# Diffusion and convolution of the next quad placed between the LSTM steps of the current one

## The chip, the cores and the metric

The kernel runs on one core of a Trainium2 chip. The metric is the device time of one execution in microseconds (us), as the median of several runs. All arithmetic is fp32; products that matter are made from two fp32r halves ("high" and "low"), three matmuls each.

## The reference

`x` holds 16 graphs (called batches below) of 512 nodes with 128 features, `adj` is one 512 x 512 matrix. Four layers follow each other; each ends with `x = layernorm(x + layer(x))` over the features.

```
L0: h = x @ fc.T + b;  8 times: h += (1/8) * (alph/2 * (adj @ h - h) + h @ w_eff - h + x0)
L1: h = relu(adj @ (x @ Wg0 + bg0));  h = relu(adj @ (h @ Wg1 + bg1))
    for p in 1..4: windows of p successive nodes go through an LSTM of their own
                   (Wih[p-1], Whh[p-1]); its last state replaces the window's last node
L2: graph convolution, linear 128->256, batchnorm, relu, linear 256->128, batchnorm
L3: edge attention with 4 heads over 256 edges, softmax by source node, W_out
```

L0 to L2 work on `x` as it comes out of the layer before. L0 and L1 need nothing of the other batches; L2's batchnorm needs all of them.

## The kernel before

A batch lies in the tile `X` as four chunks of 128 nodes. Four batches are a quad, and there are four quads. Each phase is a block with a barrier at its end.

1. `phase_operators` (L85) loads everything and makes the powers of the diffusion operator, `LT` and `E`, so that the eight Euler steps become one polynomial.
2. `phase_diffusion` (L651) does L0 for all quads. For each batch it turns `X` over and multiplies it with two powers of the operator (Y, 4 PSUM tiles), then combines these with `E` (B, 4 tiles). For each quad come two Horner steps over four batches at once (T and S, 4 tiles each). All eight PSUM banks are one ring. ScalarE (ACT) copies the high part of each tile out, VectorE (DVE) subtracts for the low part and frees the bank. GpSimd (POOL) makes low parts of what lies in SBUF and the scales of layernorm.
3. `phase_recurrent` (L888) does L1. Its weights are transposed and split once and stay in SBUF. The two graph convolutions go through a ring of four banks (4 to 7); the LSTM uses banks 0 to 3, one for each gate.
4. `phase_batchnorm` and `phase_attention` do L2 and L3.

**The LSTM of a quad** has 22 steps, numbered here from 0: four for p = 1 (one for each batch, 512 columns), then for p = 2, 3, 4 two half quads times p time steps (512, 340 and 256 columns). On TensorE (PE) a step has two parts. `from_input` multiplies the split input (`xh`, `xl`) with the input weights, and `from_state` (only for t > 0) the split state (`hh`, `hl`) with the state weights. ACT evaluates the gates, DVE makes the cell and the state. The split input of step k + 1 is made while step k runs: ACT copies `xh` at the start of its part of step k (`split_h`, L1220; where step k + 1 begins a new p, after two of the gates), POOL then subtracts for `xl`, and PE waits for it ahead of `from_input(k + 1)`.

**What sets the order.** The order of each engine's work is written out by `schedule` (L1004). It puts pieces of the convolution of the next quad between `from_input(k)` and `from_state(k)` (for t = 0 behind the step), as many pieces as the list `FILL` says; a piece is one chunk's product, of which four make a tile:

```
FILL = [1, 2, 3, 1, 2, 4, 1, 5, 3, 3, 1, 0, 1, 4, 3, 2, 0, 0, 0, 1, 1, 0]
```

Each engine does its queue strictly in that order, and waits at its semaphores in it. The residual and the second layernorm of a quad run in steps 0 to 6 of the next: statistics at step 3, scales on POOL behind the split for step 5, and the application on DVE at step 6. Quads 1 and 2 are passes of a hardware loop; quads 0 and 3 are written out.

Of the kernel before, what the change touches and what calls it, by code (L numbers as in the profile page):

```python
# [6 lines left out]
ALU = mybir.AluOpType  # L7
# [77 lines left out]
def phase_operators(nc, sh, d):  # L85
# [13 lines left out]
    with ExitStack() as ctx:  # L99
# [46 lines left out]
        sel = sb("sel", [P, C, NE])  # L146
        ones = sb("ones", [P, P])
# [7 lines left out]
                 "u_done", "xh_done", "i_in", "iota_done", "perm_done", "g_done", "deg_done",  # L155
# [25 lines left out]
        def _(sp):  # L181
# [8 lines left out]
            for q in range(sh.NB // QB):  # L190
                for c in range(C):
                    sp.dma_start(sh.X[:, c, q * QB:(q + 1) * QB, :], xv[:, c, q * QB:(q + 1) * QB, :])\
                        .then_inc(S["x_in"], 16)
            sp.wait_ge(S["x_in"], 16 * C * (sh.NB // QB))

        @block.gpsimd
        def _(pool):
# [17 lines left out]
            for c in range(C):  # L215
                pool.wait_ge(S["xh_done"], c + 1)
                low_part(pool, sh.Xl[:, c, :, :], sh.X[:, c, 0:QB, :], sh.Xh[:, c, :, :])

        @block.scalar
        def _(act):  # L220
# [34 lines left out]
        def _(dve):  # L255
# [140 lines left out]
            dve.tensor_copy(sh.ss[:, :, :], bank("PERM").rearrange("p (j e) -> p j e", j=2)).then_inc(S["dve_tile"], 1)  # L396
            low_bias("T'", 1)
            dve.wait_ge(S["dve_tile"], at["T'"] + 1)
            for c in range(C):
                ins = dve.tensor_scalar(Gs[:, c, :], sh.ss[:, 0, :], sh.ioc[:, c:c + 1], None, ALU.is_equal)  # L400
            ins.then_inc(S["g_done"], 1)
            for c in range(C):
                dve.tensor_scalar(Gd[:, c, :], sh.ss[:, 1, :], sh.ioc[:, c:c + 1], None, ALU.is_equal)
# [16 lines left out]
            copy("DROW", sh.drow[:, :], bank("DROW"))  # L420
# [230 lines left out]
def phase_diffusion(nc, sh, d):  # L651
# [3 lines left out]
    C, D, N = sh.C, sh.D, sh.N  # L655
    NQ = sh.NB // QB
    with ExitStack() as ctx:
        sb, sem = allocators(nc, ctx)
        Xh, Xl = sh.Xh, sh.Xl
        norm = sh.norm  # L660
        yh = sb("yh", [P, 2, BABY, N], F32R)
        yl = sb("yl", [P, 2, BABY, N], F32R)
        B2h = sb("B2h", [P, C, QB, D], F32R)
        B2l = sb("B2l", [P, C, QB, D], F32R)
        B01 = sb("B01", [P, C, QB, 2, D])
        tq = sb("tq", [P, C, QB, D])
        th = sb("th", [P, C, QB, D], F32R)
        tl = sb("tl", [P, C, QB, D], F32R)
        names = ("pe_tile", "dve_tile", "hi_done", "xh_done", "xl_done", "xb_done", "th_done", "tl_done",
                 "sum2", "stat_done", "norm_own", "rstd_done", "x1_done")  # L670
        S = {n: sem("d_" + n) for n in names}

        work = [("B", 0), ("Y", 2), ("B", 1), ("Y", 3), ("B", 2), ("B", 3), ("Y+", 0), ("T", 0), ("Y+", 1),
                ("S", 0)]
        TILES = 4 * len(work)
        HEAD = 8
        HIS = {"Y": 3, "Y+": 3, "B": 4, "T": 0, "S": 0}  # L680
        HI_QUAD = sum(HIS[k] for k, _ in work)
        HI_HEAD = 6

        def steps(g, last):

            hi = 0
            for i, (kind, b) in enumerate(work):
                if not (last and kind == "Y+"):
                    skipped = sum(k == "Y+" for k, _ in work[:i]) if last else 0
                    yield kind, b, HEAD + g * TILES + 4 * (i - skipped), 4 * (i - skipped) % 8, \  # L690
                        HI_HEAD + g * HI_QUAD + hi
                    hi += HIS[kind]

        block = ctx.enter_context(nc.Block())

        def ready(eng, n, k):

            eng.wait_ge(S["pe_tile"], n + k + 1)

        @block.tensor  # L700
        def _(pe):
            def free(n, k, first=False):

                if not first:
                    pe.wait_ge(S["dve_tile"], n + k - 7)

            def Y(b, n, bk, first=False):
                for k in range(4):
                    free(n, k, first)
                    o = sh.psum[:, bk + k, :]  # L710
                    if k < 2:
                        src = (Xh, Xl)[k]
                        for c in range(C):
                            ins = pe.transpose(o[:, c * P:(c + 1) * P], src[:, c, b, :].bitcast(F32),
                                               sh.ident[:, :])
                    else:
# [1581 lines left out]
```

## Time and profile before

| | us |
|---|---|
| median of 3 runs (1188.17 to 1189.53) | 1189.31 |
| the profiled execution: span | 1186.6 |
| what lies around the span (median less span) | 2.7 |
| PE busy | 998.1 |
| DVE busy | 665.5 |
| ACT busy | 584.8 |
| POOL busy | 361.7 |

The profiled execution is known by its span, from the first to the last instruction; 2.7 us lie between that and the median of the runs shown. "Busy" for PE is modelled from the starts of matmuls. The stages in the span are: operators 0 to 89.3, diffusion 89.3 to 385.4, set-up and first convolution of the recurrent phase to 433.0, its four LSTM quads to 541.6, 653.6, 769.8 and 873.9, then batchnorm and attention to 1186.6.

### The profile page before, as it was taken

The page shows a single profiled execution, that of the slowest core. Times are in us where ns is not written, and L with a number is a line of the kernel's source. Part 1 is how long each engine was busy: PE and PEld are TensorE (multiplying, and loading weights), DVE is VectorE, ACT ScalarE, POOL GpSimd, SP SyncE. Part 2 cuts the span into 40 slices and gives each one's busy share as a digit, 9 for nine tenths or more (in the row PEclk, how much of TensorE's full clock was granted, in tenths as well). Part 3 has the DMA queues.
Part 4 walks back from the last instruction along what each step waited for, and adds up shares of the span by engine and source line. Part 5 has one row for each costly group of instructions (what it writes and reads, how often), then busy time and mean ns, then how long its engine had stood idle before and what let it go on. Part 6 is the DMA issues. An engine that isn't in the chain of part 4 may idle for free. (4 is left out here: it accounts for less than half of the span.)

```text
span 1186.6 us, 15771 instructions
## 1 busy us (share of the span) xinstructions
PE 998.1 (84%) x5056; PEld 830.2 (70%) x5056; DVE 665.5 (56%) x1422; ACT 584.8 (49%) x1215; POOL 361.7 (30%) x480
## 2 busy tenths in 40 slices
PE   4989999999997788998899789968878966468694
PEld 2678989899896666886688568846856743346483
DVE  4832242342424454677567656756784478744686
ACT  2112314325241375666467646664646567664356
POOL 0021124132221322124322332242224335553156
PEclk9989999999999899999999889987898989689797
DMA  7000000000000300000000000000000000000004
GB/s 190 1 1 1 1 1 0 0 0 0 0 1 1 70 1 1 1 1 1 1 1 1 1 0 0 1 0 1 1 16 1 0 1 1 1 1 0 1 17 127
DMA packets 28700, 13.07 MB, mean 11 GB/s; under 512 B 8032, under 2 KB 27616, under 8 KB 28640
## 3 DMA queue, kind: packets, MB, share of 16 engines
q1 hardware_dynamic: 27680, 12.28, 4.1%
q8 instruction: 28, 0.46, 0.2%
q14 instruction: 32, 0.26, 0.1%
q10 hardware_dynamic: 960, 0.07, 0.1%
HBM read 8.15 MB, written 4.19 MB: 10 GB/s over the span
## 5 line engine op out<-in xcount | busy, mean ns | idle before, releaser
L1252 ACT ACTIVATE gates<-psum,gbias 128x256 f32<-128x256 f32 (+2 forms) x312 | 158.2, 564 | 55.5 <-PE psum L67 54.8
L65 PE MATMUL psum<-xh,WIh 128*128 128x256 f32 (+2 forms) x312 | 117.5, 377 | 56.3 <-POOL xl L72 53.0
L72 POOL TENSOR_TENSOR xl<-Hq,xh 128x256 fp32r<-128x256 f32 (+2 forms) x72 | 74.7, 1038 | 248.1 <-ACT xh L1233 248.1
L65 PEld LDWEIGHTS psum<-xh,WIh 128*128 128x128 f32 x312 | 63.5, 204 | 80.9 <-POOL xl L72 73.0
L67 PE MATMUL psum<-xh,WIl 128*128 128x256 f32 (+2 forms) x312 | 109.9, 352 | 0.0
L66 PE MATMUL psum<-xl,WIh 128*128 128x256 f32 (+2 forms) x312 | 109.7, 352 | 0.0
L647 ACT ACTIVATE X<-X,nshift,nscale 128x128 f32<-128x128 f32 (+1 forms) x180 | 72.0, 483 | 21.4 <-POOL nshift L587 21.4
L1256 ACT ACTIVATE tc<-cell 128x512 f32<-128x512 f32 (+2 forms) x88 | 45.2, 513 | 54.0 <-DVE cell L1345 42.7
L67 PEld LDWEIGHTS psum<-xh,WIl 128*128 128x128 f32 x312 | 63.9, 205 | 5.9
L66 PEld LDWEIGHTS psum<-xl,WIh 128*128 128x128 f32 x312 | 64.1, 205 | 4.4
L781 ACT ACTIVATE yh<-psum 128x512 fp32r<-128x512 f32 x48 | 28.6, 599 | 73.8 <-PE psum L67 72.9
L67 PE MATMUL psum<-Eh,yl 128*128 128x384 f32 x192 | 64.3, 335 | 0.0
L65 PE MATMUL psum<-Eh,yh 128*128 128x384 f32 x192 | 64.3, 335 | 0.0
L66 PE MATMUL psum<-El,yh 128*128 128x384 f32 x192 | 64.2, 334 | 0.0
L72 DVE TENSOR_TENSOR yl<-psum,yh 128x512 fp32r<-128x512 f32 x32 | 22.1, 692 | 67.8 <-ACT yh L781 67.8
L65 PE MATMUL psum<-hh,WHh 128*128 128x256 f32 (+2 forms) x192 | 59.8, 311 | 0.0
L67 PE MATMUL psum<-hh,WHl 128*128 128x256 f32 (+2 forms) x192 | 59.8, 311 | 0.0
L66 PE MATMUL psum<-hl,WHh 128*128 128x256 f32 (+2 forms) x192 | 59.8, 311 | 0.0
L72 DVE TENSOR_TENSOR B2l<-psum,B2h 128x128 fp32r<-128x128 f32 x64 | 18.6, 291 | 72.6 <-ACT B L801 70.2
L607 DVE BATCH_NORM_STATS2 nstats<-X 128x6 f32<-128x128 f32 (+1 forms) x256 | 56.4, 284 | 3.1 <-DVE X L850 1.3
L800 ACT ACTIVATE B2h<-psum 128x128 fp32r<-128x128 f32 x64 | 17.8, 278 | 74.6 <-PE psum L67 74.6
L1339 DVE TENSOR_TENSOR cell<-gates 128x512 f32<-128x512 f32 (+2 forms) x40 | 28.7, 718 | 38.5 <-ACT gates L1252 37.8
(390 smaller groups left out, 2947.6 us busy)
## 6 DMA issues: line engine op xcount, KB each, us to landing
X<-in_x SPq DMA_DIRECT2D x16, 256.0 KB, 5.1
out<-X SPq DMA_DIRECT2D x32, 128.0 KB, 1.9
A<-in_adj SPq DMA_DIRECT2D x1, 1024.0 KB, 6.3
whh<-in_L_gnn_Whh SPq DMA_DIRECT2D x1, 768.0 KB, 8.8
O<-in_L_gnn_W SPq DMA_DIRECT2D x2, 128.0 KB, 2.2
ir<-in_L_gnn_src SPq DMA_DIRECT2D x1, 128.0 KB, 6.1
ir<-in_L_gnn_dst SPq DMA_DIRECT2D x1, 128.0 KB, 6.5
Wg<-in_L_gnn_Wg SPq DMA_DIRECT2D x2, 64.0 KB, 1.9
```

What stands on the lines that cost most here:

```text
L65: pe.matmul(out, lhs[0], rhs[0], start=start, stop=False)
L66: pe.matmul(out, lhs[0], rhs[1], start=False, stop=False)
L67: return pe.matmul(out, lhs[1], rhs[0], start=False, stop=stop)
L72: return eng.tensor_tensor(out, full, high.bitcast(F32), ALU.subtract)
L607: return dve.bn_stats(self.stats[:, bass.ds(self.sh.C * n + c, 1), :], self.sh.X[:, c, bass.ds(n, 1), :])
L647: ins = act.activation(row, row, ACT.Identity, bias=shift[:, k:k + 1], scale=scale[:, k:k + 1])
L781: act.activation(yh[:, b % 2, r, :], sh.psum[:, bk + k, :], ACT.Copy)\
L800: act.activation(B2h[:, c, b, :], sh.psum[:, bk + c, 2 * D:3 * D], ACT.Copy)
L1252: act.activation(gates[:, gate, 0:n], sh.psum[:, gate, 0:n], ACT.Tanh if gate == G else ACT.Sigmoid, bias=gbias[:, p_ - 1, gate:gate + 1]) ...
L1256: act.activation(tc[:, 0:n], cell[:, s % 2, 0:n], ACT.Tanh).then_inc(S["tanh_done"], 1)
L1339: dve.tensor_tensor(c_, gates[:, I, 0:n], gates[:, G, 0:n], ALU.mult).then_inc(S["c_done"], 1)
```

## The change

`phase_diffusion` and `phase_recurrent` become one `phase_main`, with one order of work for all engines, unrolled without loops. A prologue does diffusion and convolution of quad 0, with the transposing of weights between. Then, for quad q, 22 groups that make up diffusion and convolution of quad q + 1 stand one at each LSTM step. Quad 3 has no filling. The diffusion works by pairs of batches, in the same ring of four banks as the convolution.

```diff
+        def taps(q, b):
+            return [("xt", q, b)] + [("y", q, b, r, c) for r in (1, 2) for c in range(C)] \
+                + ([("xs", q, b + 1)] if b < QB - 1 else [])
+        def back(q, b):
+            return [("b", q, b, c) for c in range(C)] + [("xb", q, b)]
+        def giant(kind, q, a):
+            made = [(kind, q, a, j) for j in (0, 1)]
+            return made + ([("th", q, a)] if kind == "t" else [("st1", q, a)])
+        def mix(q, b, layer):
+            return [("c", q, b, layer, c) for c in range(C)]
+        def weigh(q, b, layer):
+            return [("v", q, b, layer)] + ([("relu", q, b)] if layer == 0 else [])
+        def convolve(q):
+            return [[("xs", q, 4)] + mix(q, 0, 0) + [("xs", q, 5)], giant("s", q, 1),
+                    mix(q, 1, 0) + [("ln1", q, 1)] + weigh(q, 0, 0), mix(q, 0, 1) + weigh(q, 1, 0),
+                    mix(q, 1, 1) + weigh(q, 0, 1) + [("ap1", q, 1), ("xs", q, 6)], mix(q, 2, 0) + [("xs", q, 7)],
+                    weigh(q, 1, 1) + mix(q, 3, 0), weigh(q, 2, 0) + mix(q, 2, 1), weigh(q, 3, 0) + weigh(q, 2, 1),
+                    mix(q, 3, 1), weigh(q, 3, 1)]
+        def groups(q):
+            return [[("xs", q, 0)] + taps(q, 0), back(q, 0), taps(q, 1), back(q, 1), giant("t", q, 0), taps(q, 2),
+                    giant("s", q, 0), back(q, 2) + [("ln1", q, 0)], taps(q, 3), [("ap1", q, 0)] + back(q, 3),
+                    giant("t", q, 1)] + convolve(q)
+            for k_ in range(NS):
+                late = {2: [("r", q_ - 1, 0), ("r", q_ - 1, 1)], 3: [("r", q_ - 1, 2), ("r", q_ - 1, 3)],
+                        5: [("st2", q_ - 1)], 6: [("ln2", q_ - 1)], 8: [("ap2", q_ - 1)]}.get(k_, []) if q_ else []
+                middle = [("L", q_, k_)]
+                order += [("X", q_, k_)]
+                order += filling[k_] + late + middle if steps[k_][1] else middle + filling[k_] + late
...
@@ POOL, item xb
+            def add_bias(q, b):
+                n = QB * q + b
+                pool.wait_ge(S["ring_free"], ring["b", q, b, C - 1] + 1)
+                xb = sh.X[:, :, n, :]
+                pool.tensor_tensor(xb, xb, sh.bias0[:, :, :], ALU.add).then_inc(S["xb_bias"], 1)
+                pool.wait_ge(S["xb_bias"], n + 1)
+                pool.tensor_tensor(xb, xb, B01[:, :, b % 2, 0, :], ALU.add).then_inc(S["xb_done"], 1)
@@ POOL, item th
+            def giant_low(q, a):
+                for j in (0, 1):
+                    pool.wait_ge(S["th_done"], 2 * (2 * q + a) + j + 1)
+                    low_part(pool, B2l[:, chunks(j), :, :], B01[:, chunks(j), :, 1, :], B2h[:, chunks(j), :, :])
@@ POOL, item L
+                elif kind == "L":
+                    q, k = at
+                    if k < NS - 1:
+                        split_h(q, k + 1)
@@ PE, items t and s
+            def horner(kind, q, a, j):
+                n = ring[kind, q, a, j]
+                if kind == "t" and j == 0:
+                    pe.wait_ge(S["ring_free"], ring["b", q, 2 * a + 1, C - 1] + 1)
+                if kind == "s" and j == 0:
+                    pe.wait_ge(S["tl_done"], 2 * (2 * q + a) + 2)
@@ SP, the weights (512 KB a load)
+            for q in range(NQ):
+                sp.wait_ge(gate_mm[O], NS * q + end_step(1))
+                load("WI", 2)
+                if q == NQ - 1:
...
+                    sp.dma_start(sh.A[:, :, :], d["adj"].rearrange("(c p) m -> p c m", p=P)).then_inc(sh.a_again, 16)
+                sp.wait_ge(gate_mm[O], NS * q + end_step(2))
+                load("WI", 3)
+                load("WH", 1)
+                sp.wait_ge(gate_mm[O], NS * q + end_step(3))
+                if q < NQ - 1:
+                    load("WI", 0)
+                load("WH", 2)
@@ phase_batchnorm, SP
+            sp.dma_start(sh.ss[:, :, :].rearrange("p j e -> p (j e)"), sh.edges.broadcast_to([P, 2 * sh.NE]))\
+                .then_inc(S["ss_in"], 16)
+            sp.dma_start(sh.drow[:, :], sh.degrees.broadcast_to([P, N])).then_inc(S["drow_in"], 16)
@@ phase_batchnorm, DVE, ahead of its first instruction
+            dve.wait_ge(S["drow_in"], 16)
```

The items: `xs` splits one batch of X (ACT copies, POOL subtracts; one buffer, used by four diffusion and four convolution splits a quad), `xt` and `y` are the three tiles of Y (X is turned over once, not its two halves), `b` the four tiles of B, `xb` the bias and the lowest term, now on POOL, `t`, `s` and `th` the Horner steps of a pair and the split between them, `st1`, `ln1`, `ap1` statistics, scales and application (ACT) of the first layernorm of a pair, `c` and `v` the products with `adj` and with the weights, `relu` and `r` as before, `st2`, `ln2`, `ap2` the second layernorm. `X` and `L` are `from_input` and `from_state`. In the prologue DVE waits for all set-up loads, the biases `bi` and `bh` (the last two of SP's eight) among them, ahead of its first item. Of the seven weight blocks two input ones and one state one have a place in SBUF; all are written to DRAM in the prologue and loaded again for each p. `adj` is overwritten by the states of even quads and loaded again in quad 3. The edge rows and the degree row go through DRAM.

## Rows read from the trace of the kernel before

**Rows 1.** Windows: stretch, length, busy PE, PEld, DVE, ACT, POOL, clock, DMA, GB/s
```profile
89.30:385.40 296.10, 289.60 (x1472) 257.52 (x1473) 99.51 (x224) 94.84 (x253) 71.92 (x83) 1.00 0.00 0
385.40:433.00 47.60, 39.51 (x199) 32.04 (x199) 24.93 (x46) 21.89 (x46) 11.75 (x18) 0.89 0.21 44
433.00:541.60 108.60, 98.39 (x541) 83.21 (x542) 64.85 (x114) 72.44 (x139) 29.77 (x26) 0.97 0.00 1
541.60:653.60 112.00, 98.53 (x553) 83.24 (x552) 77.52 (x153) 69.63 (x139) 36.74 (x39) 0.98 0.00 1
653.60:769.80 116.20, 102.61 (x552) 86.08 (x551) 77.55 (x153) 69.86 (x138) 36.76 (x39) 0.94 0.00 0
769.80:873.90 104.10, 78.70 (x408) 67.67 (x406) 69.43 (x139) 61.26 (x123) 29.14 (x34) 0.85 0.00 1
873.90:1186.60 312.70, 221.89 (x1047) 169.61 (x1047) 201.94 (x450) 177.95 (x353) 137.85 (x216) 0.86 0.06 15
```

**Rows 2.** The same view, of one stretch that holds only B products
```profile
102.07:108.24 6.17, 6.17 (x37) 6.14 (x36) 1.57 (x4) 2.26 (x7) 0.00 (x0) 1.00 0.00 1
```

**Rows 3.** Waits, 433 to 874 us; columns: total us, times, longest
```profile
PEld psum L65 <- POOL xl L72: 73.0, 57, 5.3
```

**Rows 4.** Timeline around step 6, second quad; columns: start, us, then what
```profile
582.52 0.39 PE L65 MATMUL psum<-hh,WHh 128*128 128x512 f32 x1
...
582.72 0.60 ACT L1272 ACTIVATE ych<-psum 128x512 fp32r<-128x512 f32 x1 [7.89 <-PE psum L67]
...
583.21 0.66 ACT L1233 ACTIVATE xh<-Hq 128x512 fp32r<-128x512 f32 x1
...
583.95 1.31 POOL L72 TENSOR_TENSOR xl<-Hq,xh 128x512 fp32r<-128x512 f32 x1 [6.63 <-ACT xh L1233]
...
585.32 0.50 PE L65 MATMUL psum<-xh,WIh 128*128 128x512 f32 x1
```

**Rows 5.** Timeline of PE at step 16, `from_state` to the next step
```profile
633.44 0.28 PE L65 MATMUL psum<-hh,WHh 128*128 128x256 f32 x1
...
634.86 0.28 PE L65 MATMUL psum<-xh,WIh 128*128 128x256 f32 x1
```

**Rows 6.** Timeline where POOL makes sixteen scales ahead of a split
```profile
567.77 0.69 POOL L572 TENSOR_TENSOR nwork<-nstats 128x16 f32 x1
...
576.03 1.29 POOL L72 TENSOR_TENSOR xl<-Hq,xh 128x512 fp32r<-128x512 f32 x1
...
576.11 5.14 DVE L626 TENSOR_SCALAR X<-X,nscale,nshift  x16 [1.94 <-POOL nshift L587]
...
577.37 0.50 PE L65 MATMUL psum<-xh,WIh 128*128 128x512 f32 x1 [3.71 <-POOL xl L72]
```

**Rows 7.** Timeline of POOL: scales of eight columns, first and last
```profile
1171.56 0.21 POOL L572 TENSOR_TENSOR nwork<-nstats 128x8 f32<-128x8 f32 x1
...
1175.65 0.20 POOL L587 TENSOR_TENSOR last_shift<-last_mean,nwork 128x8 f32<-128x8 f32 x1
```

**Rows 8.** Timeline at the start of the second quad
```profile
547.14 2.70 POOL L72 TENSOR_TENSOR rXl<-X,rXh 128x512 fp32r<-128x512 f32 x2 [1.93 <-ACT rXh L1214]
...
548.47 0.50 PE L65 MATMUL psum<-ATh,rXh 128*128 128x512 f32 x1 [0.80 <-POOL rXl L72]
```

**Rows 9.** Groups by line and form, diffusion; busy us, mean ns, idle before
```profile
L801 ACT ACTIVATE B<-psum 128x256 f32<-128x256 f32 x64 | 24.5, 382 | 0.0
...
L647 ACT ACTIVATE X<-X,nshift,nscale x32 | 12.5, 483 | 0.0
```

**Rows 10.** DMA issues of the page; KB each, us to landing
```profile
whh<-in_L_gnn_Whh SPq DMA_DIRECT2D x1, 768.0 KB, 8.8
```

**Rows 11.** Timeline of the queue of SP, last issue of the recurrent set-up
```profile
392.76 3.74 SPq L1089 DMA_DIRECT2D bh<-in_L_gnn_bhh  x1
```

**Rows 12.** Timeline of DVE: one product beside a running POOL split, one alone
```profile
549.82 1.81 DVE L1339 TENSOR_TENSOR cell<-gates 128x512 f32<-128x512 f32 x1
...
561.54 0.69 DVE L1339 TENSOR_TENSOR cell<-gates 128x512 f32<-128x512 f32 x1 [0.40 <-ACT gates L1252]
```

More of the change, by code:

```diff
@@ new lines, in phase_main @@
+        order = prologue()
+        for q_ in range(NQ):
+            filling = groups(q_ + 1) if q_ < NQ - 1 else [[] for _ in range(NS)]
+            assert len(filling) == NS
+            for k_ in range(NS):
[4 more added lines that the diff above has]
+                order += filling[k_] + late + middle if steps[k_][1] else middle + filling[k_] + late
@@ new lines, in phase_main @@
+        order += [("r", NQ - 1, b) for b in range(QB)]
+        ring, high = {}, {}
+        for item_ in order:
+            kind_ = item_[0]
+            if kind_ in ("xt", "b", "t", "s", "v", "r"):
+                name_ = item_
+            elif kind_ in ("y", "c") and item_[4] == C - 1:
+                name_ = item_[:4]
+            else:
+                continue
+            ring[name_] = len(ring)
+            if kind_ in ("xt", "y", "b", "c"):
+                high[name_] = len(high)
@@ L1284, in _ @@
[L1284 to L1285 removed]
+                act.wait_ge(S["c_done"], NS * q + k + 1)
+                act.activation(tcs[:, 0:n], cell[:, s % 2, 0:n], ACT.Tanh).then_inc(S["tanh_done"], 1)
             act.wait_ge(S["g_in"], 64)
             for i in (0, 1):
[L1288 to L1291 removed]
@@ L1292, in _ @@
-            run(schedule(0, True, False), 0, True)
-            with act.Fori(1, NQ - 1) as g:
-                run(schedule(g, True, True), g, True)
-            run(schedule(NQ - 1, False, True), NQ - 1, False)
+                act.activation(Wgs[i][0][:, :], Wg[i], ACT.Copy).then_inc(S["wg_hi"], 1)
+            for item in order:
+                kind, at = item[0], item[1:]
+                if kind == "set":
+                    set_up(*at)
+                elif kind == "xs":
+                    split_x(*at)
+                elif kind == "xt":
+                    taps_high(*at, 0)
+                elif kind == "y" and at[-1] == C - 1:
+                    taps_high(*at[:3])
+                elif kind == "b":
+                    combined(*at)
+                elif kind == "th":
+                    giant_high(*at)
+                elif kind == "ap1":
+                    apply_first(*at)
+                elif kind == "c" and at[-1] == C - 1:
+                    conv_high(*at[:3])
+                elif kind == "relu":
+                    conv_relu(*at)
+                elif kind == "first":
+                    split_h(0, 0)
+                elif kind == "L":
+                    lstm(*at)
```

1091 lines of the change are left out of this document (497 added, 594 removed).

## The prediction

> **What bounds the kernel now.** I read the windows by stage first [rows 1]. Diffusion is PE alone: 289.6 us of 296.1 busy at clock 1.00, so about 74.0 us a quad, and nothing waits. The LSTM quads are different. Quads 0 to 2 take 108.6, 112.0 and 116.2 us with PE busy for 98.4, 98.5 and 102.6; the last, without filling, takes 104.1 with 78.7 busy and a clock of 0.85. ACT, the next engine, is busy for 70 us a quad. So PE bounds the filled quads too, less its waits, and the waits view says which: in 433 to 874 us PE's weight loads wait 73.0 us in 57 cases for `xl` of POOL [rows 3]. This is the wait ahead of `from_input(k + 1)`.
>
> The timeline shows how that wait is made. At [rows 4] a filling ends in a finished tile at 582.5. ACT copies the tile out first, then makes `xh`, then POOL makes `xl` (1.31), and `from_input` starts at 585.32: 2.8 us after the filling's end. PE is not idle there only because `from_state` with 512 columns takes just these 2.80 us. With 256 columns it takes 1.42 [rows 5], and the same chain (0.2 to ACT, 0.5 for the tile, 0.7 for `xh`, some 0.9 for a shorter `xl`) takes 2.3. Where POOL has something else ahead of `xl`, PE waits for that as well: sixteen scales (8.3 us from 567.77 to 576.03) ahead of a split cost PE 3.7 us idle [rows 6].
>
> What the filling can win is therefore what PE idles now: 10.2, 13.5 and 13.6 us in the filled quads, 25.4 in the last. What it can lose is new waits of PE, since every engine keeps its order and PE now has filling enough that any wait is time.
>
> **Work of PE.** Diffusion brings 289.6/4 = 72.4 us a quad. X is turned over once instead of twice: 16 transposes fewer, at most 0.17 each by the larger product of [rows 2] (6.17/36), so I take 2 off: 70.4. The Horner steps by pairs are twice as many products of 256 columns; 1.42/12 = 0.118 [rows 5] against half of 2.80/12 = 0.233 [rows 4], no difference. Three filled quads: 299.5 + 3 x 70.4 = 510.7 us of PE, against 3 x 74.0 + 336.8 = 558.9 us of span now. If no wait were left, 48 us would be won there.
>
> **Waits of a filled quad.** I walk along PE with durations from the rows: an eviction of 512 columns by ACT 0.6 (0.5 start to start), one b tile 0.7 (0.38 of it for the lower terms [rows 9]) and 1.54 on PE [rows 2], DVE's low part 0.7 (0.3 for a b tile), POOL 1.3 for 512 elements [rows 4, 6], 1.1 and 0.9 for narrow ones, 4.3 for eight scales [rows 7], 0.39 for one application by ACT (12.5/32) [rows 9], 5.1 for sixteen by DVE [rows 6].
>
> - Step 0. The first split of X of the next quad stands behind the tanh of step 0. Now POOL begins it 547.14 - 541.6 = 5.5 us after the quad's first product, two chunks in 2.7, and PE starts on it at 548.47 [rows 8]. With 1.3 for one batch it is there at 6.8; PE has 2.1 + 0.4 to do. Wait 4.3.
> - Step 6 to 7. `ln2` stands ahead of the split on POOL, as in [rows 6], with more of PE's work beside it: 2.0 (nothing to 3.7).
> - Step 7 to 8. Behind the last b tile come ACT 0.9, DVE 0.3, then on POOL two bias additions 2.6, `ln1` 4.3, and only then `xl` 1.1: 9.2 us, against 2.8 of `from_state`. Wait 6.4.
> - Step 10. The first t tile needs the last b tile freed. From the last y tile: evictions 1.4, `ap2` on DVE 5.1, the cell and tanh of step 9 1.2, `ap1` on ACT 3.1, four b evictions 2.4, DVE 0.4: 13.6, against 1.4 + 6.2 + 1.8 on PE. Wait 4.2.
> - Step 10 to 11. Behind the last t tile: DVE 0.9, ACT, POOL's two low parts of the pair to 4.1, `xl` 1.1, less `from_state` 1.8: 3.4.
> - Step 11. `xs` 4 stands behind the tanh (0.5), `xs` 5 ahead of `xl` on POOL (2.0): 2.5.
> - Steps 13 and 15: a split that needs two gates first, and `relu` between `v` and `c`: 2.2 + 1.2.
> - Step 16. `ap1` 3.1 and `xs` 6 stand behind the tile on ACT: 3.6, then `xs` 7 ahead of `xl`: 2.0.
> - Steps 17 to 20: the bare chain four times (2.3 - 1.42, say 0.8), and `relu` once 2.2: 5.4.
>
> Sum 37.2. Quad 0 has no second layernorm: about 32. Three quads: 106 us. From both sides: the waits would halve (53) if ACT and POOL ran ahead of PE where I have them behind, and the DVE additions that lie near POOL's may lengthen them by a third (141). I take 106, which is the nearest to the rows. 510.7 + 106 = 616.7, against 558.9: **+57.8**.
>
> One rule bears on the size of these waits. One DVE product took 1.81 us beside a running split of POOL and 0.69 alone [rows 12]. The Trainium skill, page "SBUF — State Buffer", section "Who interferes with whom", has an exclusive lock between the two engines (for an instruction of DVE with two inputs in SBUF and one of POOL that reads SBUF), so that the later instruction waits for the whole of the earlier; by it the some 20 new instructions of POOL in a quad could hold DVE for 1.1 us each, and the waits would be nearer to 141 than to 106. A second rule of the Trainium skill speaks for the change: the page "Runtime: NRT & Kernel Launch", section "Instruction fetch mechanics", prefers straight code to taken branches. The looped quads take 3.4 and 7.6 us more than the unrolled quad 0 [rows 1]; if all of that were fetching, the sum would be 11 lower.
>
> **Prologue.** Now: 74.0 + 47.6 (set-up and first convolution) = 121.6 us. After: 70.4 + 39.5 of PE, some 3 less for the slow clock of 0.89 there, 107. DVE waits for `bh`, whose issue now ends at 396.5, 11.1 us behind the block's start [rows 11], and must still land; PE has the first y tiles and `adj` to turn over, and waits 7.5 in all by the end of the second batch. Then t tiles behind b 2, the pair's split with `ap1` and `xs` 4 4.7, three `relu` chains and a last tile 9, `ap1` and `xs` 6 4.6, `xs` 7 1.5. Two state weight blocks follow each other in one buffer, so ACT waits for the first to be written to DRAM; 768 KB took 8.8 us to land [rows 10], 512 KB some 5, which costs 2.8. In all 32: 139, **+17.4** (from 0 to 25).
>
> **The rest.** The last quad keeps its form; its loads of 2 x 512 KB have three `from_input` parts and two chains, some 10 us, until `from_state(10)` needs them: +1 (0 to 8). DVE's first work in batchnorm now waits for two broadcasts from DRAM, which it had in SBUF: +5 (2 to 8.8, [rows 10]). The DMAs at the end of the operators lie beside the last logarithm: 0 to 2.
>
> **Sum** on the profiled execution: 1186.6 + 57.8 + 17.4 + 1 + 5 = 1267.8, with the 2.7 around the span 1270.5. I forecast **1270 us**, slower by 7%.
>
> **Rivals.**
> 1. *The filling covers the waits* (faster). The 57 waits for `xl` are short, and 70.4/22 = 3.2 us of new work of PE a step would hide each, were ACT and POOL ahead. For it: the second quad idles 13.5 us in 22 steps even with DVE, ACT and POOL busy to two thirds. Against it: the filling stands before `from_state`, and the split of step k + 1 behind the filling on ACT, so it does not cover this chain but lengthens it. With the present prologue cost it gives 1186.6 - 48.2 + 23.4 + 2.7 = 1164. It decides from 24.8 us of waits downwards in the three quads, 8 a quad. Chance 0.08.
> 2. *Half of the waits.* The long ones at steps 8, 10 and 16 stand, the others overlap: 1270.5 - 53 - 8 = 1209. For it: at [rows 5] nothing stands between two parts of PE, though the chain of 2.3 us is longer than the part of 1.42. Chance 0.22.
> 3. *The clock goes as well.* PE is busy for 76% of the last quad and has 0.85 of the full clock, against 88% and 0.98 in the second [rows 1]. Waits of 4 to 6 us leave the new quads at some 83%. Were all their 510.7 us at 0.85 instead of 0.96, 66 more: 1336; half of it 1303. Chance 0.13.
> 4. *Streamed weights come late*, so that the filling doesn't do its work: two waits a quad of up to 8.8 us, 1186.6 + 81.2 + 53 + 2.7 = 1324. The nearest need is some 10 us behind its load, in filled quads 20. Chance 0.02.
>
> **How the numbers follow.** 0.55 for the forecast, the rest as given. The range goes from 1205 (rival 2) to 1315 (rival 3 by half, and the upper bound of the waits). A difference of 0.2% is what a measurement of this kernel can tell from none. Faster 0.09, from rival 1 and a little of rival 2's lower side; within 0.2% 0.01; slower 0.90.
>
> **What would show it.** Right: one pass from the first `from_input` of a quad to that of the next of 195 to 210 us; PE waiting 4 us or more for POOL's `xl` ahead of the p = 3 steps (step 8), at t tiles for b tiles, and at the fifth and seventh X split; POOL's scales and bias additions just ahead of `xl`; a prologue near 139 us. Wrong: filled quads under 175 us, PE busy above 95% in them; or a wait of PE for a DMA of weights; or waits of equal sum in other places, which would make the time right for the wrong reason.

## The result, and the profile after

The changed kernel takes 1302.79 us (median of 4 runs, 1300.62 to 1306.16) against 1189.42 for the kernel before (1188.17 to 1194.12): a ratio of 1.095 (95% interval 1.092 to 1.098), slower by 9.5%. The forecast was slower by 7% (1270 us, range 1205 to 1315). The profiled execution has a span of 1298.6 us and a granted clock of 0.903 over all.

The windows by stage of the kernel after answer to [rows 1]: operators; prologue (diffusion and convolution of quad 0, set-up); the three filled quads; the last quad; batchnorm and attention. Columns are length, then busy us and count for PE, PEld, DVE, ACT, POOL, then clock, DMA share, GB/s.

```profile
0.00:89.90 89.90, 69.78 (x299) 51.64 (x300) 49.74 (x148) 14.84 (x23) 2.74 (x21) 0.94 0.24 63
89.90:237.10 147.20, 119.71 (x645) 104.07 (x644) 45.34 (x99) 42.60 (x99) 34.84 (x48) 0.91 0.13 40
237.10:448.00 210.90, 178.84 (x982) 159.46 (x983) 89.91 (x166) 95.81 (x205) 61.50 (x68) 0.92 0.04 13
448.00:663.10 215.10, 180.77 (x1001) 161.03 (x1000) 101.10 (x206) 95.04 (x208) 66.64 (x81) 0.92 0.05 18
663.10:878.10 215.00, 180.74 (x1001) 160.95 (x1000) 101.10 (x205) 94.96 (x207) 66.65 (x81) 0.92 0.05 18
878.10:982.00 103.90, 75.67 (x412) 65.63 (x410) 66.67 (x137) 62.22 (x124) 30.36 (x34) 0.89 0.12 41
982.00:1298.60 316.60, 222.72 (x1047) 170.70 (x1047) 200.36 (x451) 178.10 (x353) 137.45 (x216) 0.86 0.06 17
```

Length less PE busy is what PE idles: 32.1, 34.3 and 34.3 us in the filled quads, where the kernel before has 10.2, 13.5 and 13.6 [rows 1] and idles 6.5 more in all 296 us of diffusion. Beside that stands the clock: 0.92 in every filled quad, where diffusion had 1.00 and the quads 0.97, 0.98 and 0.94.

The timeline of POOL, PE and some of DVE around step 8 of the second filled quad shows the longest wait. It is [rows 6] over again, with more ahead of the split.

```profile
526.84 1.29 POOL L1370 TENSOR_TENSOR X<-X,bias 128x512 f32<-128x512 f32 x1 [10.47 <-DVE B2l L72]
...
528.21 1.60 POOL L1372 TENSOR_TENSOR X<-X,B 128x512 f32<-128x512 f32 x1
...
529.13 1.23 DVE L1298 TENSOR_TENSOR gates<-gates,cell 128x512 f32<-128x512 f32 x1 [0.43 <-ACT gates L1163]
529.78 0.65 POOL L571 TENSOR_TENSOR n1work<-nstats 128x8 f32<-128x8 f32 x1
530.39 0.21 POOL L572 TENSOR_TENSOR n1work<-nstats 128x8 f32<-128x8 f32 x1
...
530.39 0.75 DVE L1300 TENSOR_TENSOR cell<-gates 128x512 f32<-128x512 f32 x1
530.56 0.65 POOL L573 TENSOR_TENSOR n1work<-nstats 128x8 f32<-128x8 f32 x1
...
531.84 0.69 DVE L1304 TENSOR_TENSOR Hodd<-gates,tc 128x512 f32<-128x512 f32 x1 [0.70 <-ACT tc L1167]
531.89 0.70 POOL L577 TENSOR_TENSOR n1work<-n1work,const 128x8 f32<-128x8 f32 x1
...
533.39 1.64 POOL L583 TENSOR_TENSOR n1work<-n1work,const 128x8 f32<-128x8 f32 x1
...
535.42 1.00 POOL L72 TENSOR_TENSOR LS<-Hodd,LS 128x340 fp32r<-128x340 f32 x1
...
536.52 0.62 PE L65 MATMUL psum<-LS,WI 128*128 128x340 f32 x1 [7.88 <-issue]
...
537.51 0.49 PE L65 MATMUL psum<-LS,WI 128*128 128x340 f32 x1
```

Two bias additions and the thirteen instructions that make eight scales take POOL from 526.84 to 535.42, the split follows, and PE, idle for 7.88 us, starts when it ends. (The row says "issue", but POOL's split ended at 536.42.) And then the products run slowly: 0.49 us for 340 columns. Windows of the same place show the granted clock before, in and behind the wait:

```profile
524.00:528.00 4.00, 4.00 (x21) 3.57 (x20) 0.58 (x2) 2.52 (x7) 1.16 (x1) 1.00 0.00 0
528.00:536.50 8.50, 0.64 (x3) 0.20 (x2) 3.37 (x4) 2.30 (x4) 7.87 (x16) 0.66 0.34 124
536.50:540.00 3.50, 3.48 (x14) 3.44 (x14) 0.51 (x1) 1.94 (x4) 0.20 (x1) 0.50 0.02 5
```

0.50 is the lower level, 1.2 GHz of 2.4: this wait is paid a second time in the work behind it. So are shorter ones: in the 4 us behind the waits of 4.08 and 3.79 us shown below the granted clock is 0.60 and 0.50. The Trainium skill, page "Perfetto Trace Analysis", section "Matmul Optimizations", says that the matmul engine scales its power with its utilisation, so matmuls should come back to back in batches; these windows agree.

Four more of PE's waits in that quad, and the one of the last quad (timeline of PE, the wait in brackets):

```profile
454.83 0.47 PE L65 MATMUL psum<-LT0h,XSh 128*128 128x512 f32 x1 [4.08 <-POOL XSl L72]
...
558.53 0.58 PE L65 MATMUL psum<-B2h,LT2h 128*128 128x256 f32 x1 [2.53 <-DVE B2l L72]
...
570.98 0.42 PE L65 MATMUL psum<-LS,WI 128*128 128x340 f32 x1 [3.38 <-POOL LS L72]
...
617.39 0.76 PE L65 MATMUL psum<-ATh,XSh 128*128 128x512 f32 x1 [3.79 <-POOL XSl L72]
...
915.41 0.80 PE L65 MATMUL psum<-LS,WI 128*128 128x512 f32 x1 [10.25 <-POOL LS L72]
```

The fourth, at step 16, on ACT and POOL: eight applications stand ahead of the split of X.

```profile
611.51 0.60 ACT L1123 ACTIVATE yh<-psum 128x512 fp32r<-128x512 f32 x1 [1.72 <-PE psum L67]
612.00 3.18 ACT L1117 ACTIVATE X<-X,n1shift,n1scale 128x128 f32<-128x128 f32 x8
615.27 0.63 ACT L1089 ACTIVATE XSh<-X 128x512 fp32r<-128x512 f32 x1
615.98 1.26 POOL L72 TENSOR_TENSOR XSl<-X,XSh 128x512 fp32r<-128x512 f32 x1 [6.92 <-ACT XSh L1089]
```

The streamed weights are no part of this. They land in the 3.6 and 4.5 us of the page's section of DMA issues, and of the waits between 89.9 and 982 us only those of set-up loads and of one write in the prologue are for a DMA:

```profile
WI<-lstm_weights SPq DMA_DIRECT2D x14, 512.0 KB, 3.6
WH<-lstm_weights SPq DMA_DIRECT2D x11, 512.0 KB, 4.5
```

```profile
DVE gbias L1328 <- DMA bh<-in_L_gnn_bhh: 7.7, 1, 7.7
...
ACT WH L1082 <- DMA lstm_weights<-WH: 3.5, 1, 3.5
```

### The profile page after: what moved, and what is told of

Same layout as the page of the kernel before. It is cut to its first block and busy times, and to the rows that moved or that the text cites. A ratio compares the mean times of both kernels' runs of the same rounds, so it can differ in the third digit from the quotient of the medians.

```text
span 1298.6 us, 15636 instructions
## 1 busy us (share of the span) xinstructions
PE 1028.2 (79%) x5376; PEld 873.5 (67%) x5376; DVE 654.2 (50%) x1406; ACT 583.6 (45%) x1215; POOL 400.2 (31%) x548
## 5 line engine op out<-in xcount | busy, mean ns | idle before, releaser
L65 PE MATMUL psum<-LS,WI 128*128 128x256 f32 (+2 forms) x312 | 116.4, 373 | 86.3 <-POOL LS L72 58.5
L65 PEld LDWEIGHTS psum<-LS,WI 128*128 128x128 f32 x312 | 64.9, 208 | 103.3 <-POOL LS L72 62.1
L72 DVE TENSOR_TENSOR yl<-psum,yh 128x512 fp32r<-128x512 f32 x74 | 50.7, 690 | 163.2 <-ACT yh L1123 115.5
L66 PE MATMUL psum<-LS,WI 128*128 128x256 f32 (+2 forms) x312 | 110.5, 354 | 0.0
L67 PE MATMUL psum<-LS,WI 128*128 128x256 f32 (+2 forms) x312 | 110.3, 354 | 0.0
L72 POOL TENSOR_TENSOR XSl<-X,XSh 128x512 fp32r<-128x512 f32 x32 | 41.8, 1307 | 195.4 <-ACT XSh L1089 195.4
L72 POOL TENSOR_TENSOR LS<-A,LS 128x512 fp32r<-128x512 f32 (+2 forms) x44 | 49.9, 1135 | 128.5 <-ACT LS L1141 128.5
L72 POOL TENSOR_TENSOR LS<-Hodd,LS 128x512 fp32r<-128x512 f32 (+2 forms) x44 | 49.3, 1120 | 118.4 <-ACT LS L1141 118.4
L65 PE MATMUL psum<-B2h,LT2h 128*128 128x256 f32 x256 | 73.7, 288 | 5.2 <-DVE B2l L72 5.0
L66 PE MATMUL psum<-B2l,LT2h 128*128 128x256 f32 x256 | 73.0, 285 | 0.0
L67 PE MATMUL psum<-B2h,LT2l 128*128 128x256 f32 x256 | 73.0, 285 | 0.0
L67 PEld LDWEIGHTS psum<-LS,WI 128*128 128x128 f32 x312 | 65.7, 211 | 5.0
L66 PEld LDWEIGHTS psum<-LS,WI 128*128 128x128 f32 x312 | 65.6, 210 | 4.1
L65 PE MATMUL psum<-LS,WH 128*128 128x256 f32 (+2 forms) x192 | 60.7, 316 | 0.0
L66 PE MATMUL psum<-LS,WH 128*128 128x256 f32 (+2 forms) x192 | 60.2, 314 | 0.0
L67 PE MATMUL psum<-LS,WH 128*128 128x256 f32 (+2 forms) x192 | 60.1, 313 | 0.0
L67 PE MATMUL psum<-Eh,yl 128*128 128x384 f32 x168 | 56.7, 338 | 0.0
```

Source lines behind the costliest of these rows:

```text
L65: pe.matmul(out, lhs[0], rhs[0], start=start, stop=False)
L66: pe.matmul(out, lhs[0], rhs[1], start=False, stop=False)
L67: return pe.matmul(out, lhs[1], rhs[0], start=False, stop=stop)
L72: return eng.tensor_tensor(out, full, high.bitcast(F32), ALU.subtract)
```

## The experiments

Theories after the result. **A**: the waits are those of the order in which ACT and POOL get their work, the clock follows from them, and other orders take both away. **B**: the clock, or this kind of work (more matmuls of 256 columns, weights loaded for each), makes PE slow by itself. **C**: setting diffusion between the LSTM steps is what costs. **D**: the streamed weights cost through something that the waits view doesn't name.

The runs side by side, first: the second filled quad of each, from windows (us; idle is length less busy).

| kernel | median | ratio (95%) | quad | PE busy | idle | clock |
|---|---|---|---|---|---|---|
| after | 1302.8 | 1.095 (1.092–1.098) | 215.1 | 180.8 | 34.3 | 0.92 |
| no_stream | 1301.4 | 1.095 (1.092–1.097) | | | | |
| pool_behind | 1270.2 | 1.068 (1.066–1.071) | 205.1 | 177.0 | 28.1 | 0.95 |
| split_ahead | 1256.6 | 1.057 (1.054–1.059) | 200.7 | 177.8 | 22.9 | 0.94 |
| warm | 1280.6 | 1.077 (1.075–1.079) | 205.9 | 194.8 | 11.1 | 1.00 |
| apart | 1383.9 | 1.164 (1.162–1.167) | 245.8 | 189.1 | 56.7 | 0.90 |
| reorder_only | 1221.9 | 1.028 (1.026–1.030) | 191.5 | 170.1 | 21.4 | 0.99 |
| reordered | 1173.9 | 0.988 (0.985–0.990) | 177.8 | 167.9 | 9.9 | 1.00 |
| best1 | 1169.7 | 0.984 (0.982–0.987) | 177.9 | 168.1 | 9.8 | 1.00 |
| before_split | 1186.1 | 0.997 (0.996–0.999) | | | | |

**pool_behind.** POOL's bias additions, lower terms, scales and trailing splits of X stand behind its split for step k + 1; nothing else moves.

```diff
+        def behind_split(items):
...
+                        def needed(m):
+                            return seg[m][0] not in ("xb", "th", "ln1", "ln2") and not (
+                                seg[m][0] == "xs" and not any(s_[0] in ("y", "c") for s_ in seg[m + 1:]))
+                        out += [s_ for m, s_ in enumerate(seg) if needed(m)] + [it] \
+                            + [s_ for m, s_ in enumerate(seg) if not needed(m)]
@@ block.gpsimd
-            for item in order:
+            for item in behind_split(order):
```

> The changed kernel with one difference on POOL alone: where filling stands ahead of from_state, the items that nothing of that filling needs (bias additions, low parts of a Horner pair, scales, the trailing split of X) stand behind the split of step k + 1 instead of ahead of it. Theory 1 (the order puts waits on PE's path): of the waits of a filled quad, step 8 falls from 8.05 to about 1.2 us, step 7 loses its 0.5, step 11 falls from 3.5 to 2.1, step 12 from 1.8 to 1.3, step 17 from 2.05 to 1.4: some 10 us a quad, with a share of the slow clock 13, so about 1302.8 - 39 = 1264 us. Theory 2 (the loss is in what the pipeline does besides: weights from DRAM, the pairs, straight code, a lower clock whatever the waits): within 5 us of 1303.

Measured 1270.19 us (1269.33 to 1272.88), 32.6 less. The timeline of POOL and PE at the same step 8:

```profile
527.18 1.00 POOL L72 TENSOR_TENSOR LS<-Hodd,LS 128x340 fp32r<-128x340 f32 x1 [12.81 <-ACT LS L1164]
528.14 1.74 POOL L1393 TENSOR_TENSOR X<-X,bias 128x512 f32<-128x512 f32 x1
...
528.28 0.39 PE L65 MATMUL psum<-LS,WI 128*128 128x340 f32 x1 [1.05 <-issue]
528.51 0.32 PE L66 MATMUL psum<-LS,WI 128*128 128x340 f32 x1
...
538.22 0.42 PE L65 MATMUL psum<-LS,WI 128*128 128x340 f32 x1 [2.26 <-POOL LS L72]
```

The wait of 7.88 is 1.05, and the products behind it take 0.32 instead of 0.49. Part of it came back: the scales now stand ahead of the split of step 9, which waits 2.26, and for the fifth split of X PE now waits 3.92 us, where it waited 0.35. The theory holds; it forecast 39 us less and got 32.6, because these waits came in.

**split_ahead.** As pool_behind, and ACT (so POOL too) splits the hidden state for step k + 1 already at `from_input(k)`, ahead of the filling's evictions, where t > 0 and the next step's input exists.

```diff
+        def ahead(k):
+            return steps[k][1] > 0 and (k == NS - 1 or steps[k + 1][1] > 0)
@@ ACT
-                if k < NS - 1 and not late:
+                if k < NS - 1 and not late and not ahead(k):
                     split_h(q, k + 1)
+                elif kind == "X" and ahead(at[1]):
+                    if at[1] < NS - 1:
+                        split_h(at[0], at[1] + 1)
...
```

> As the kernel with POOL's items behind the split, and on both ACT and POOL the split of step k + 1 is made at from_input(k), ahead of the filling, wherever t > 0 and step k + 1 does not begin a new p. Theory 1: the remaining chain (eviction, xh, xl) behind each filling leaves PE's path: steps 11, 12 and 17 to 21 lose 2.1 + 1.3 + 1.4 + 3.7 = 8.5 us more a quad, with the clock's share some 10: about 1233 us. Theory 2: no further change. A third view, that ACT would then be late with the evictions and the ring of four banks would stop PE instead, gives waits of PE ahead of ring tiles and 1260 us or more.

1256.64 us (1254.42 to 1258.55): 13.6 less, not 37. The bare chains went, but the splits of X and the tiles behind them became what is late (timeline of PE, step 11):

```profile
557.46 0.77 PE L65 MATMUL psum<-ATh,XSh 128*128 128x512 f32 x1 [4.67 <-POOL XSl L72]
```

The filled quad idles 5.2 us less, but PE is busy for 177.8, as in pool_behind (177.0), at a clock of 0.94: four waits of more than 2.5 us are left, 4.08, 4.67 and 3.79 for a split of X and 2.88 for a low part of DVE. The timeline puts none of them down to a free bank of the ring, so the third view was not the reason, though its time came near.

**apart.** The whole filling stands behind step 21 instead of between the steps, with the same work and order within it; the first input split of the next quad stands behind it. This tests C.

```diff
-                order += filling[k_] + late + middle if steps[k_][1] else middle + filling[k_] + late
+                order += late + middle if steps[k_][1] else middle + late
+            order += [item for group in filling for item in group] + ([("next", q_ + 1)] if q_ < NQ - 1 else [])
```

> The changed kernel without its interleaving: all 22 groups of the next quad stand behind step 21 of the current one, in their order; first input split of the next quad behind them. Everything else (pairs, ring of four, streamed weights, straight code) stays. Theory 1: interleaving as such still wins, since an unfilled LSTM quad takes 104 us and diffusion with convolution alone about 133 (the prologue's 147 less its set-up), together some 237 against 215: about 1370 us. Theory 2 (the interleaving itself loses, the parts alone are as good as in the kernel before): 186 a quad, about 1210 us.

1383.91 us (1383.44 to 1385.37). C falls: the interleaving is worth 31 us a quad (245.8 against 215.1), in an order that is far from good.

**no_stream.** The weights are not loaded again, and PE doesn't wait for them; the states then use whatever block lies in the buffer. It leaves out the 25 loads of 512 KB; the load of `adj` stays.

```diff
-                load("WI", 2)
...
-                if k == first_step(p_):
-                    wait(pe, wi_in[slot], 16 * (2 * q + (p_ > 2)))
-                if t == 1 and s == 0:
-                    wait(pe, S["wh_in"], 16 * (3 * q + p_ - 2))
```

> The changed kernel without the loads of streamed LSTM weights from DRAM and the waits for them; it then computes steps with whatever weights lie in the buffers (the writes to DRAM in the prologue stay). Theory 1: streaming is hidden, PE waits for no such load: 1300 to 1304 us. Theory 2, weights that come late or take bandwidth from the engines: 10 to 50 us less, 1250 to 1293.

1301.40 us (1299.74 to 1302.97), within the error of the kernel after. D falls.

**warm.** PE makes 110 extra matmuls a quad of 512 constant columns (10% more PE work) where it waits for the long ones; the target is overwritten by the work that follows.

```diff
+            def keep_busy(out, m):
+                for _ in range(m):
+                    pe.matmul(out, sh.LT[2][0][:, 0, 0:P], sh.LT[2][0][:, 0, :], start=True, stop=True)
@@ from_input
+                filler = {8: 30, 11: 12, 12: 6, 14: 7, 17: 7}.get(k, 0) if q < NQ - 1 else 0
@@ first y, second t, and both weight products of batch 2: 16, 9, 15, 8
```

> The changed kernel with extra matmuls of constant data (128x512, into a PSUM bank that the next real product of PE overwrites) set where PE waited: per quad 16 ahead of the first y tile (quads 1 and 2), 9 ahead of the second pair's t tile, 15 and 8 ahead of two convolution tiles (all in diffusion and convolution of quads 1 to 3), and 30, 12, 6, 7 and 7 ahead of the input products of steps 8, 11, 12, 14 and 17; some 110 a quad, 25 us more of PE's work, nearly all inside waits that stay. What is left out of the result: nothing. Theory 1 with the clock (of 215 us a filled quad, PE idles 38 and loses some 12 to the slow clock that follows the waits): the granted clock of the filled quads rises from 0.92 to about 0.98 and a quad loses 8 to 10 us, less 1 to 2 where an extra matmul overshoots: about 1280 us. Rival (the 12 us are not the clock but contention or modelled ends, or extra work delays PE): 1303 to 1320.

1280.58 us (1278.99 to 1281.05), 22.2 less with more work. Windows of the quad, of the filled wait at step 8, and of what follows it:

```profile
443.68:649.58 205.90, 194.80 (x1111) 171.25 (x1109) 101.20 (x205) 94.91 (x207) 66.84 (x81) 1.00 0.06 19
...
524.00:530.50 6.50, 5.52 (x25) 4.24 (x23) 1.93 (x3) 0.63 (x1) 6.03 (x14) 1.00 0.40 153
530.50:540.00 9.50, 9.38 (x48) 7.99 (x49) 4.31 (x8) 5.12 (x11) 1.51 (x3) 1.00 0.00 0
```

ACT's and POOL's order is as in the kernel after, and the useful work starts again no earlier than POOL lets it; only the clock differs, 1.00 instead of 0.66 and 0.50. The extra matmuls are 110 x 0.233 = 25.6 us (5.83 us for 25 of them in the timeline), so the useful work falls from 180.8 to 169.2 us; idle time and extra work together are 36.7 where the kernel after idles 34.3. The net 9.2 us a quad is the clock's share, bought back. B falls too: this kind of work runs at full clock once the waits are filled.

**reordered.** split_ahead, and the filling's long items stand elsewhere: the first split of X of the next diffusion at step 19 of the quad before, the fifth at step 10, `ln1` a step later, `ap1` of the second pair with the split behind it a step earlier, and two weight products of the convolution a step earlier. In the prologue one weight block stands behind the third group of the convolution instead of ahead of `ap1`.

```diff
-            return [[("xs", q, 4)] + mix(q, 0, 0) + [("xs", q, 5)], giant("s", q, 1),
-                    mix(q, 1, 0) + [("ln1", q, 1)] + weigh(q, 0, 0), mix(q, 0, 1) + weigh(q, 1, 0),
-                    mix(q, 1, 1) + weigh(q, 0, 1) + [("ap1", q, 1), ("xs", q, 6)], mix(q, 2, 0) + [("xs", q, 7)],
-                    weigh(q, 1, 1) + mix(q, 3, 0), weigh(q, 2, 0) + mix(q, 2, 1), weigh(q, 3, 0) + weigh(q, 2, 1),
-                    mix(q, 3, 1), weigh(q, 3, 1)]
+            nxt = [("xs", q + 1, 0)] if q < NQ - 1 else []
+            return [mix(q, 0, 0) + [("xs", q, 5)], giant("s", q, 1),
+                    mix(q, 1, 0) + [("ln1", q, 1)] + weigh(q, 0, 0),
+                    mix(q, 0, 1) + weigh(q, 1, 0) + [("ap1", q, 1), ("xs", q, 6)],
+                    mix(q, 1, 1) + weigh(q, 0, 1), mix(q, 2, 0) + [("xs", q, 7)],
+                    weigh(q, 1, 1) + mix(q, 3, 0) + weigh(q, 2, 0), mix(q, 2, 1) + weigh(q, 3, 0),
+                    nxt + weigh(q, 2, 1), mix(q, 3, 1), weigh(q, 3, 1)]
@@ groups
-            return [[("xs", q, 0)] + taps(q, 0), ...
-                    giant("s", q, 0), back(q, 2) + [("ln1", q, 0)], taps(q, 3), [("ap1", q, 0)] + back(q, 3),
-                    giant("t", q, 1)] + convolve(q)
+            return [taps(q, 0), ...
+                    giant("s", q, 0), back(q, 2), [("ln1", q, 0)] + taps(q, 3), [("ap1", q, 0)] + back(q, 3),
+                    [("xs", q, 4)] + giant("t", q, 1)] + convolve(q)
```

> As the kernel with the splits ahead, and seven items of the filling moved: the first X split of the next quad from step 0 to step 19 of the quad before, the first pair's scales one group later, the fourth X split from step 11 to 10, the second pair's application with its X split from step 15 to 14, the weight products of batches 2 and 3 a group earlier than the mix that needs them, and one weight block of the prologue later. Theory 1: the waits of 26 us a quad lose 4.2 (start), 2.4 (step 9), 4.8 (step 11), 3.9 (step 16), 3.0 (relu), so some 8 stay, the slow clock goes from 10 to 6, a quad takes some 179 us instead of 200.7, and the prologue loses 6: about 1256.6 - 65 - 6 = 1186 us. Theory 2, that waits only move to other places because POOL or ACT is the real bound: above 1230.

1173.90 us (1171.88 to 1177.31): 82.7 below split_ahead, and 1.2% faster than the kernel before. The quad, by windows:

```profile
400.62:578.41 177.79, 167.90 (x998) 150.97 (x999) 103.19 (x205) 94.65 (x208) 66.36 (x81) 1.00 0.06 22
```

It has the same matmuls as split_ahead, in 167.9 us instead of 177.8. Step 8's wait is down to 1.05 us. The longest left is the t tile's; then come 1.92 and 1.44 us:

```profile
495.92 0.39 PE L65 MATMUL psum<-B2h,LT2h 128*128 128x256 f32 x1 [2.64 <-DVE B2l L72]
```

**reorder_only.** The moves of reordered without the other two edits: do the gains add?

> The changed kernel with the moves of filling items alone (as in the reordered version), POOL's order and the place of ACT's split as in the changed kernel. First theory (the gains add: POOL's order 32.6 us, the early split 13.6, the moves 82.7): 1302.8 - 83 = 1220. Second theory (POOL's long items ahead of the split set the waits whatever the filling's order, so the moves gain little by themselves): above 1255. Third (the moves alone take every long wait, and the other two edits are worth little once they are there): below 1195. I hold with 1220.

1221.90 us (1220.71 to 1225.46), 80.9 below after, where the same moves take 82.7 off split_ahead: they add. Its quad answers a second question. It idles nearly as long as that of split_ahead (21.4 and 22.9) and yet has a clock of 0.99:

```profile
416.39:607.87 191.48, 170.05 (x1001) 152.00 (x999) 102.16 (x205) 94.76 (x207) 66.40 (x81) 0.99 0.06 20
```

So it isn't the sum of idle time alone that sets the clock; pool_behind says the same, with 28.1 us of idle time and 0.95. Its longest waits are 3.37, 2.68 and 2.55 us, where split_ahead has 4.67, 4.08, 3.79 and 2.88. But the length of a wait doesn't settle it alone either. The longest here, and the shortest of those four, with the windows of what follows each (reorder_only, then split_ahead):

```profile
524.98 0.42 PE L65 MATMUL psum<-LS,WI 128*128 128x340 f32 x1 [3.37 <-POOL LS L72]
...
525.00:529.00 4.00, 4.00 (x21) 3.63 (x22) 2.18 (x5) 0.49 (x1) 0.00 (x0) 1.00 0.00 0
```

```profile
619.11 0.76 PE L65 MATMUL psum<-ATh,B2h 128*128 128x512 f32 x1 [2.88 <-DVE B2l L1290]
...
619.00:623.00 4.00, 3.89 (x9) 3.13 (x10) 0.00 (x0) 0.00 (x0) 0.00 (x0) 0.50 0.00 0
```

Behind 3.37 us of waiting the clock stays at 1.00, behind 2.88 it is 0.50. Which waits cost the clock, and what else decides it, was not tried one by one and stays open.

**best1.** reordered, and in the prologue ACT's split of the graph weights and DVE's sum of the gate biases stand where they are first needed, not ahead of everything.

```diff
@@ ACT, ahead of the first set-up item behind adj (before: ahead of all items)
+                if item == ("set", C):
+                    act.wait_ge(S["g_in"], 64)
...
@@ DVE, ahead of b(0, 0) and of the first split of the states (before: ahead of all items)
+                if kind == "first":
+                    dve.wait_ge(S["b_in"], 32)
+                    dve.tensor_tensor(gbias[:, :, :], bi[:, :, :], bh[:, :, :], ALU.add)\
...
```

> As reordered, and in the prologue ACT's split of the convolution weights and DVE's sum of the LSTM biases stand where they are needed, so that the first X split doesn't wait for the weight load and DVE not for the last of SP's loads. Theory 1: the first wait of 5.0 us falls to about 1.5 and the next of 1.1 goes: 4 to 5 us less than reordered, about 1181.

1169.69 us (1164.55 to 1172.93), the fastest of all: 0.984 of the kernel before (0.982 to 0.987). Against reordered it is 4.2 us less, with ranges that overlap, so this edit alone is not well shown. The profiled execution is the fastest of the four (span 1162.6 us, the others about 1168 to 1171). Its windows (prologue, three quads, last quad, the rest):

```profile
89.90:217.14 127.24, 112.75 (x647) 98.84 (x645) 46.79 (x98) 43.27 (x100) 36.03 (x49) 0.99 0.15 46
217.14:392.29 175.15, 167.38 (x982) 150.62 (x983) 92.54 (x167) 95.89 (x206) 61.34 (x68) 0.99 0.05 16
392.29:570.19 177.90, 168.07 (x998) 151.11 (x999) 103.29 (x205) 94.70 (x208) 66.27 (x81) 1.00 0.06 22
570.19:749.89 179.70, 169.39 (x999) 152.16 (x999) 102.97 (x205) 94.39 (x207) 64.86 (x80) 0.99 0.06 21
749.89:846.70 96.81, 75.34 (x410) 65.52 (x410) 67.90 (x137) 61.87 (x124) 30.70 (x34) 0.89 0.14 44
846.70:1162.60 315.90, 222.19 (x1047) 169.65 (x1047) 200.60 (x450) 178.35 (x353) 138.00 (x216) 0.86 0.06 17
```

The three quads take 532.8 us where the kernel before takes 558.8 for the same work (336.8 and three times 74.0); the prologue costs 5.6 more than before, the last quad 7.3 less, and batchnorm and attention 3.2 more.

**before_split.** Was the early split to be had without the change? The kernel before, with this edit alone.

> The kernel before, with one edit alone: ACT's (and so POOL's) split of the hidden state for step k + 1 stands at from_input(k), ahead of the filling's evictions, where t > 0 and the next step's input exists. It asks whether the repair of the new kernel was to be had without the change. First theory (the bare chain of 2.3 to 2.8 us behind a filling makes most of the 13 us that PE idles in a looped quad): at 12 or so steps a quad up to 1 us less, some 6 us a filled quad and 4 in the last, 1165 to 1175. Second theory (from_state covers the chain already where it has 512 columns, and the other waits of a quad are the sixteen scales and the splits of X, which stay): 1183 to 1190. I hold with 1176.

1186.14 us (1184.02 to 1188.53), ratio 0.997: 2.7 us. I held with 1176; the second theory has it. Its three filled quads idle 9.7, 11.8 and 15.2 us by windows, where the kernel before idles 10.2, 13.5 and 13.6, so the early split takes next to nothing off them; best1 is 16 us below it. Whether moves of the filling would help the kernel before as well was not tried.

## Why the prediction was right in its sign and 33 us short

**The waits were right.** I predicted 37.2 us of waits for a filled quad with a second layernorm. The table gives the gaps between PE's starts in the second filled quad, less the usual time from start to start; they sum to 37.1. Each is some 0.16 us more than the wait that the timeline shows in brackets, and by windows the quad idles 34.3. They lie where the walk had them, though single ones are off by up to 1.7 us both ways, so that a sum this close is partly luck:

| place | predicted | measured |
|---|---|---|
| step 0, first split of X | 4.3 | 4.25 |
| step 6 to 7, `ln2` | 2.0 | 0.55 |
| step 7 to 8, bias and `ln1` | 6.4 | 8.05 |
| step 10, t tile | 4.2 | 2.69 |
| step 10 to 11 | 3.4 | 3.54 |
| step 11, `xs` 4 and 5 | 2.5 | 0.68 + 1.84 |
| steps 13 and 15 | 2.2 + 1.2 | 2.08 + 1.31 |
| step 16, `ap1` and `xs` 6, `xs` 7 | 3.6 + 2.0 | 3.95 + 2.05 |
| steps 17 to 20, `relu` once | 5.4 | 4 x 0.92 + 2.43 |

At step 6 to 7 POOL had more time than I gave it. At step 8 POOL began as assumed: PE left the last b tile at 525.69 and the first addition started at 526.84, 1.15 us later, where I had 1.2. The additions took 2.94 us where I had 2.6, the split 1.00 where I had 1.1. The scales took 5.64 us, from 529.78 to 535.42, where I had 4.3, and that is most of the 1.65 us that this wait was longer. Three of the thirteen instructions took 0.65, 0.65 and 0.70 us, some 1.4 us more in all than the 0.2 that their like took in [rows 7], and each stands beside a product of DVE with two inputs in SBUF (529.13, 530.39 and 531.84 in the timeline). In windows, the three quads idle 100.7 us, where I had 106. The Trainium skill's page "SBUF — State Buffer", section "Who interferes with whom", has the lock by which I would have had nearer to 141: these three instructions agree with it, but the 141 did not come, since few such meetings lay on PE's path. No run takes the contention away alone, so the rule itself is not tested.

**PE's own time was wrong.** The failed step is the first term: 510.7 us of PE for three quads, taken at the clocks of the stages that it came from (1.00 in diffusion, 0.97, 0.98 and 0.94 in the quads; 0.98 over all). Measured are 540.4 us at 0.92: +29.7. The clocks alone would give 510.7 x 0.98/0.92, +33 (an estimate), and the same items at clocks of 0.99 to 1.00 took 504.8 us in best1. With the waits at -5.3 this makes the quads 641.0 instead of 616.7. The prologue has the same fault in part: PE busy for 119.7 us instead of 107 at a clock of 0.91, +12.7, and idle for 27.5 instead of 32; in all 147.2 instead of 139. In best1, at 0.99, its PE work takes 112.8 us, so some 7 of the 12.7 go with the clock, and 107 was too low by nearly 6 even without it; where those come from was not read. (The single waits that I wrote down for the prologue add to 30.1, not 32.) That I took PE's work over at the old clock, and put the same waits that I had just counted beside it, was a contradiction in the sum: waits of 4 to 8 us are not free of what they do to the clock. I had it as rival 3 and gave it 0.13; its "half of it 1303" is what came, on the forecast's own waits. That the number fits to the microsecond is luck: the half had no working behind it, the 0.96 that rival 3 starts from should have been the 0.98 above (some 78 us for all of it, not 66), and what was too low in the prologue's work and too high in the waits went into it unseen. The warm run shows the clock as cause of 9.2 us a quad net, 11.6 of PE's useful work, and reordered shows the same matmuls at 167.9 us, close to the 168.9 that I had for that quad.

**The other terms.** The last quad, 103.9 against 105.1 predicted; PE idles 28.2 us in it against 25.4 before [rows 1], 10.25 of them in one wait behind sixteen scales of POOL, ahead of step 7. Batchnorm: +3.9 against +5; DVE waits 5.27 us for the degree row at 987.61:

```profile
987.61 1.14 DVE L1642 SCALAR_TENSOR_TENSOR O<-ident,dinv,drow 128x128 f32<-128x128 f32 x4 [5.27 <-DMA drow<-degrees]
```

Operators +0.6, within 0 to 2. The differences, 24.3 + 8.2 - 1.2 - 1.1 + 0.6, make 30.8: from 1267.8 to the span of 1298.6.

**The rivals.** The filling covers the waits (1): wrong for this order, and right for the reordered one; its point of decision, 8 us of waits a quad, was near: reordered idles 9.9 in its second quad, at a better clock than I had put in, and is faster by 1.2%. Half of the waits (2): no. Streamed weights (4): no, by no_stream. My mark of 195 to 210 us for a quad was missed on the upper side (210.9, 215.1, 215.0), and only the clock says why.

**Open.** Of the moves in reordered none was run alone. The gain of 23 us a quad over split_ahead is 13 us of idle time and 10 of PE's busy time, at a clock of 1.00 instead of 0.94, but which item brings how much isn't settled.

## What to carry to other kernels

When filling is set between the steps of a dependent chain, walk every helper engine's queue, not PE's alone: what counts is what stands ahead of the one small instruction that PE needs next, and the same work in another order was worth 129 us here. Count long waits of PE with the slow work behind them, since its own busy time rises with them, and try filling them with constant matmuls: a profile in which that makes the kernel faster says that the clock is a term of the sum. Loading weights from DRAM again cost nothing here, where each block was there before PE needed it; how near to the use it may stand was not tried.

## What was unexpected of the hardware

Ten per cent more matmuls made the kernel 22 us faster, at a clock of 1.00 instead of 0.92. Two quads with nearly equal idle time (21.4 and 22.9 us) had clocks of 0.99 and 0.94, and a wait of 3.37 us left the clock at 1.00 where one of 2.88 us elsewhere was followed by 0.50. And 25 loads of 512 KB, at 3.6 to 4.5 us each beside a busy PE, ACT, DVE and POOL, cost nothing that a comparison can see (1301.4 against 1302.8). Instructions of 8 columns on POOL took 0.65 to 0.70 us beside products of DVE that read two tiles of SBUF, and 0.20 to 0.21 elsewhere.
